# Feed-forward products in full float32 on unsplit activations, in place of two fp32r products on high and low parts

## What is computed

```python
def _L0_ffn_ref(x, W1, b1, W2, b2):
    def _ternary(w):
        scale = jnp.maximum(jnp.mean(jnp.abs(w)), 1e-08)
        w_t = jnp.clip(jnp.round(w / scale), -1.0, 1.0)
        return w + jax.lax.stop_gradient(w_t - w)
    h = jnp.einsum('bsd,fd->bsf', x, _ternary(W1)) + b1      # 256 -> 1024
    h = jax.nn.gelu(h, approximate=False)
    out = jnp.einsum('bsf,df->bsd', h, _ternary(W2)) + b2    # 1024 -> 256
    return out
...
x = x + _layernorm(_L0_ffn_ref(_layernorm(x, axis=-1), L0_ffn_W1, L0_ffn_b1, L0_ffn_W2, L0_ffn_b2), axis=-1)
```

## Time and profile before

| | us |
|---|---|
| median of 3 runs | 2201.29 (2200.94 to 2201.91) |
| the profiled execution | 2210.3 |
| its span, first to last instruction | 2208.5 |
| PE busy in the span | 1818.8 (82%) |
| DVE busy | 1532.1 (69%) |
| ACT busy | 863.3 (39%) |
| POOL (GpSimd) busy | 709.7 (32%) |

### The profile page before, as it was taken

How to read it: one execution, slowest core, us unless ns; L and a number is a source line. 1 busy time by engine, 2 the same in 40 slices (tenths; PEclk the granted TensorE clock), 3 DMA queues, 4 the chain that set the end, 5 groups by cost and what they waited for, 6 DMA issues and landing times. The chain is left out here.

```text
span 2208.5 us, 32795 instructions
## 1 busy us (share of the span) xinstructions
PE 1818.8 (82%) x10766; PEld 1165.7 (53%) x10766; DVE 1532.1 (69%) x3312; ACT 863.3 (39%) x1846; POOL 709.7 (32%) x643
## 2 busy tenths in 40 slices
PE   4878998898899889889988988998675654499977
PEld 2544555454555545545554555554444433489953
DVE  2346696598669668866965896697589845577736
ACT  1343353343335334433533343343422213366733
POOL 0000241043014104411420340143048863467641
PEclk9589999999999999999999999999876666699989
DMA  4000000000000000000000000000113234676667
GB/s 142 1 1 10 1 2 10 11 1 1 21 1 1 11 11 1 1 20 1 1 10 11 1 1 20 1 1 1 39 50 113 83 117 159 215 231 196 191 208 267
DMA packets 83443, 119.49 MB, mean 54 GB/s; under 512 B 12665, under 2 KB 70077, under 8 KB 83136
## 3 DMA queue, kind: packets, MB, share of 16 engines
q1 hardware_dynamic: 67088, 79.43, 11.4%
q0 software_dynamic: 13056, 35.68, 4.3%
q10 hardware_dynamic: 3120, 2.06, 0.3%
HBM read 67.43 MB, written 51.79 MB: 54 GB/s over the span
## 5 line engine op out<-in xcount | busy, mean ns | idle before, releaser
L681 DVE TENSOR_TENSOR_SCAN s_buf<-r_work,kvb 128x512 f32<-128x512 f32 x256 | 361.8, 1416 | 0.0
L866 POOL TENSOR_TENSOR p_buf<-s_buf,r_work 128x512 f32<-128x512 f32 x128 | 152.3, 1190 | 457.2 <-DVE s_buf L681 447.9
L956 ACT ACTIVATE probs<-bank_s,nmx 128x256 f32<-128x256 f32 (+1 forms) x512 | 186.9, 452 | 92.1 <-DVE nmx L541 90.5
L866 POOL TENSOR_TENSOR r_work<-s_buf,r_work 128x512 f32<-128x512 f32 x128 | 158.2, 1238 | 172.3 <-DVE s_buf L681 172.0
L821 POOL TENSOR_TENSOR rstd<-vare,mhalf 128x4 f32<-128x4 f32 x48 | 48.4, 1008 | 496.5 <-DVE vare L475 496.5
L974 ACT ACTIVATE pt<-bank_s 128x1024 f32<-128x1024 f32 (+1 forms) x128 | 117.6, 918 | 230.1 <-PE bank_s L1260 230.1
L670 DVE TENSOR_TENSOR kvb<-r_work,bank 128x512 f32<-128x512 f32 x256 | 174.2, 681 | 15.7 <-PE bank L1383 6.9
L1958 POOL DMA_INDIRECT y_rows<-w_in_ys,m_y_idx x144 | 141.9, 985 | 89.0 <-ACT w_in_ys L2046 52.2
L541 DVE TENSOR_REDUCE nmx<-bank_s 128x4 f32<-128x1024 f32 (+1 forms) x128 | 137.6, 1075 | 40.1 <-PE bank_s L1210 39.3
L1382 PE MATMUL bank<-v_hi,sel_v 128*128 128x512 f32 x256 | 130.2, 508 | 21.8 <-DVE kvb L670 15.4
L1210 PE MATMUL bank_s<-kT,qT 32*128 32x256 f32 (+1 forms) x1024 | 139.1, 391 | 0.0
(11 more groups left out here) (405 smaller groups left out, 4189.5 us busy)
## 6 DMA issues: line engine op xcount, KB each, us to landing
m_xs<-x_rows SPq DMA_DIRECT2D x144, 144.0 KB
w_lo<-y_rows SPq DMA_DIRECT2D x4, 2048.0 KB, 22.6
w_hi<-y_rows SPq DMA_DIRECT2D x4, 2048.0 KB, 24.9
w_in_ys<-in_w SPq DMA_DIRECT2D x17, 256.0 KB, 3.9
x_new<-in_x SPq DMA_DIRECT2D x8, 512.0 KB, 3.8
x_after_rwkv<-x_b SPq DMA_DIRECT2D x8, 512.0 KB, 3.7
m_x_all<-x_after_rwkv SPq DMA_DIRECT2D x8, 512.0 KB, 4.5
out<-m_x_all SPq DMA_DIRECT2D x8, 512.0 KB, 3.5
```

The lines of the kernel that those rows point to most:

```text
L681: V.tensor_tensor_scan(s_buf[:, n % 2, 1:S + 1], dec[:, n // HD, :], kvb[:, n % 2, :], 0.0, ALU.mult, ALU.add).then_inc(sem["state"], 1)
L866: G.tensor_tensor(p_slot(n), s_buf[:, n % 2, 0:S], rf[:, n // HD, :], ALU.mult).then_inc(sem["rs"], 1)
L956: ins = A(probs[:, n % 2, x, h * w:h * w + w], score_banks[n % 2][:, x, h * w:h * w + w], ACT.Exp, bias=nmx[:, n, 2 * x + h:2 * x + h + 1])
```

## The change

The weights stay in their tiles and are read as float32 (`bitcast(F32)`); the moving operand is unsplit float32. `up(f)` is now 2 products from `xT` (a float32 tile that attention uses earlier in the batch), `down(f)` 2 products. ACT writes `xT` in place of `hiT`, and its gelu goes straight to one of four slots in `work`, from which PE reads. DVE's `loT` and `g_lo`, ACT's `g_hi` and the semaphores `f_lo` and `g_lo` fall away: PE's first `up` waits for `evened`, and `down(f)` for `g_hi` of f, which the gelu now signals. A slot is written again when `down(f-4)` is done.

```diff
@@ vector
-                ve.wait_ge(sem["evened"], at(b, "evened", 4))
-                for k, src in enumerate((A0, A1)):
-                    ins = V.tensor_tensor(loT[:, k, :], src[:], hiT[:, k, :].bitcast(F32), ALU.subtract)
-                ins.then_inc(sem["f_lo"], 1)
                 yield "turn2"
                 for f in range(NF + 2):
-                    if f < NF:
-                        ve.wait_ge(sem["g_hi"], at(b, "g_hi", f + 1))
-                        V.tensor_tensor(g_lo[:, f % 2, :], work[:, f % 2, :], g_hi[:, f % 2, :].bitcast(F32), ALU.subtract
-                                        ).then_inc(sem["g_lo"], 1)
                     yield f"ffn{f}"
@@ scalar
-                    A(hiT[:, k, :], src[:], ACT.Copy).then_inc(sem["evened"], 1)
+                    A(xT[:, k, :], src[:], ACT.Copy).then_inc(sem["evened"], 1)
...
-                        if f >= 2:
-                            sc.wait_ge(sem["g_lo"], at(b, "g_lo", f - 1))
-                        g_ins = A(work[:, f % 2, :], bank[f % 3][:], ACT.Gelu, bias=b1[:, f:f + 1])
-                        g_ins.then_inc(act_own, 1)
-                        if f >= 2:
-                            sc.wait_ge(sem["f_y"], at(b, "f_y", f - 1))
-                        sc.wait_ge(act_own, b * NF + f + 1)
-                        A(g_hi[:, f % 2, :], work[:, f % 2, :], ACT.Copy).then_inc(sem["g_hi"], 1)
+                        if f >= 4:
+                            sc.wait_ge(sem["f_y"], at(b, "f_y", f - 3))
+                        A(g_slot(f), bank[f % 3][:], ACT.Gelu, bias=b1[:, f:f + 1]).then_inc(sem["g_hi"], 1)
@@ tensor, up
                     for k in range(NK):
-                        for c, part in enumerate((hiT, loT)):
-                            ins = T.matmul(bank[f % 3][:], w1t[:, k, f * P:(f + 1) * P], part[:, k, :],
-                                           start=k == 0 and c == 0, stop=k == NK - 1 and c == 1)
+                        ins = T.matmul(bank[f % 3][:], w1t[:, k, f * P:(f + 1) * P].bitcast(F32), xT[:, k, :], start=k == 0, stop=k == NK - 1)
@@ tensor, down
-                    pe.wait_ge(sem["g_lo"], at(b, "g_lo", f + 1))
+                    pe.wait_ge(sem["g_hi"], at(b, "g_hi", f + 1))
                     for k, dst in enumerate((A3, A4)):
-                        for c, part in enumerate((g_hi[:, f % 2, :], g_lo[:, f % 2, :])):
-                            ins = T.matmul(dst[:], w2t[:, f, k * P:(k + 1) * P], part, start=f == 0 and c == 0,
-                                           stop=f == NF - 1 and c == 1)
+                        ins = T.matmul(dst[:], w2t[:, f, k * P:(k + 1) * P].bitcast(F32), g_slot(f), start=f == 0, stop=f == NF - 1)
@@ tensor, before the first up
                 repeat(A4, 5)
-                pe.wait_ge(sem["f_lo"], at(b, "f_lo", 1))
+                pe.wait_ge(sem["evened"], at(b, "evened", 4))
```

More of the change, by code:

```diff
@@ L59 @@
     loc=QUADS, diff=QUADS, gate_z=1, gate_e=1, mixed=1, mixed_t=2, mixed_sb=2, out_ps=1,
-    f_lo=1, h_ps=NF, g_hi=NF, g_lo=NF, f_y=NF, fy_sb=2, fy_tok=1,
+    f_lo=0, h_ps=NF, g_hi=NF, g_lo=0, f_y=NF, fy_sb=2, fy_tok=1,
     r_var=2, r_rstd=2, r_normed=NT, r_turned=NK, r_xt=NK, mix=8, proj=8, v_f=2, v_lo=1, k_f=2, dec=2, decay=1, r_f=2,
@@ L172, in mid_token_layers @@
         s_zero = ctx.enter_context(nc.semaphore("s_zero"))
-        act_own = ctx.enter_context(nc.semaphore("act_own"))
         e_const = ctx.enter_context(nc.semaphore("e_const"))
@@ L307, in p_slot, with g_slot @@
             return p_buf[:, i, :] if i < 4 else r_work[:, (0, 1, 4, 5)[i - 4], :]
+        def g_slot(f):
+            return work[:, (0, 1, 4, 5)[f % 4], :]
         def at(b, name, k):
```

## The result

The changed kernel takes 2284.39 us (median of 4 runs, 2282.57 to 2287.42) against 2201.6 us for the kernel before; the ratio is 1.0365, with a 95% interval from 1.0345 to 1.0385, that is +82.8 us between the medians. Measured once more beside the experiments it took 2288.65 us (median of 6) against 2201.69, ratio 1.0387 (1.0347 to 1.0427), +87.0 us. The forecast was 2290.6 us, +89.3. Its sign, its mechanism and its range held. What remains to be explained are a few microseconds, and whether they lie in the terms of the sum or outside them.

What follows compares the result with a forecast made beforehand. PE was taken to bound the feed-forward stage: +103.7 us for products, -9.0 for the start and -5.4 for inner waits gave +89.3, a median of 2290.6 us. The range was 2277 to 2306 us.

Steps and rivals of the forecast that it cites:

- What bounds the stage: Feed-forward stage: PE's own time bounds it, busy 21.48 of 21.90 us in batch 2 at clock 1.00.
- The unit prices: Up and down products: 0.860 us per float32 product against 0.455 per fp32r pair, 256 times, 103.7 us more.
- Rival D: Up and down products: float32 with ternary weights needs no second record, deciding at 0.51 us a product; 2129 us, chance 0.03.
- The start: Start of the stage: without loT PE starts 1.1 us earlier each batch, 9 us back in all.
- Rival B: Stage start and g_lo waits: no wait comes back, PE stays held; +103.7, 2305 us, chance 0.06.
- The waits inside: PE's waits for g_lo before down vanish: 1.2 us back in batch 0, some 0.6 in each other, 5.4 together.
- ACT, DVE, slots, the end: Work freed on ACT and DVE, slot and bank waits, and the stage's last record: each worth nothing beyond the waits.
- The RWKV chain's cover: RWKV steps behind the fourth gelu, up to L1122: PE has 8.6 us of products meanwhile, so they cost nothing.
- The estimate by the pages: Products priced by the Trainium skill's pages: 110 us more for the products, 2297 us in all.
- The clock: Iterations outside the sum: losses of 12.3 us, placed at batch borders after PE idles, drawn anew; give or take 12 us.
- Rival A: Batch borders: the clock falls badly in every iteration, 28 us more, 2319 us; chance 0.06.

Runs made afterwards that it cites:

- after_act_dve_load: Changed kernel with ACT's rounding copy and DVE's subtraction of every gelu put back as work nobody reads or waits for: 2291.1 us, ratio 1.0388.
- up_f32: Kernel before with only the up products in float32 on xT, down and the gelu's parts as before: 2244.47 us, ratio 1.0173.
- down_f32: Kernel before with only the down products in float32 from the four slots, up and loT as before: 2244.35 us, ratio 1.019.
- high_only: Changed kernel with single fp32r products on the rounded activations, low parts left out of up and down: 2152.02 us, ratio 0.9746.
- after_start_wait: Changed kernel with DVE's unread loT subtraction put back and PE waiting for it before the first up: 2293.86 us, ratio 1.0427.
- before_filled: Kernel before with unread filler products in PE's two idle stretches at each batch's borders: 2205.08 us, ratio 1.0015.
- high_first: Kernel before with PE's terms reordered, high parts running before the waits for loT and g_lo: 2188.72 us, ratio 0.9933.

## Why the prediction was right, point by point

*What bounds the stage.* Right. PE is busy in 33.69 of 33.70 us, the clock is 1.00, and work put back on the other engines does nothing (after_act_dve_load), while passes of PE added or taken away come out in the stage (up_f32, down_f32, high_only).

*The unit prices.* Right: two records for each float32 product, 0.43 us apart, with weights of -1, 0 and 1 too. Rival D is out: its point of decision was 0.51 us a product, and the product takes 0.86.

*The start.* Forecast 1.1 us a batch, measured 1.14 after the change, 1.25 with the wait put back alone. PE starts where its fillers end, as predicted. Rival B would have left 1.38 and falls.

*The waits inside.* The one term that was mis-sized: I had 5.4 us in all; the stage grew by 94.65 and not by 103.7, so 9.0 came back. Most of the missing piece is visible in the trace of before. After each wait the next record starts 0.34 us behind the first and not 0.23:

```profile
581.56 0.50 PE L1313 MATMUL bank_s<-g_hi,w2t 128*128 128x512 f32 x1 [0.37 <-DVE g_lo L617]
...
581.90 0.39 PE L1313 MATMUL bank_s<-g_lo,w2t 128*128 128x512 f32 x1
...
582.13 0.39 PE L1313 MATMUL bank<-g_hi,w2t 128*128 128x512 f32 x1
```

A restart thus costs 0.11 us beyond the idle time. Each batch has three of them, the start and two waits, 0.33 us; I was off by 0.41 in batch 0 and by 0.46 in each other. (The second wait in the loop is short, 0.05 us.) The changed kernel has no restart because it has no wait: where one was put back, in after_start_wait, its float32 product lost 0.1 us in the same way. Of the 3.6 us in all, 2.6 are restarts and 0.4 is the pace, 0.429 us a record in the changed kernel and not 0.430; 0.6 is not accounted for.

*ACT, DVE, slots, the end.* All costed at nothing, and nothing is what they cost, as far as the stages tell: PE has no idle time in them. The RWKV chain's cover of 8.6 us was real: when high_only took it away, the wait appeared.

*The estimate by the pages.* An fp32r product in a row took 0.2275 us in the trace, where the Trainium skill ("TensorE: Matmul & The Clock Gate", section "Back-to-back issue gap") has 0.216. By that figure the estimate of the products' term was 110 us. The paces in the traces, 2 x 0.429 after and 2 x 0.2275 before, give 256 x 0.403 = 103 us, and the runs side with them.

*The clock.* I kept it out of the sum as something drawn anew and gave it 12 us in either direction; that was right in kind. Two things were not. I put the loss at the borders of batches, and before_filled shows that a clock held up there saves no time. Even in the longest iteration, the one of the earlier trace rows, the records at the border lost 5.79 - 3.70 = 2.1 us of the 5.75; the rest goes with a stretch further on, where the clock was low for 10 us:

```profile
1236.00:1246.20 10.20, 10.20 (x36) 5.33 (x35) 7.35 (x9) 1.50 (x5) 3.97 (x4) 0.51 0.00 0
```

And I called 0.2% what a measurement of this kernel can tell. The three runs that I had seen lay within 1 us; in later sessions executions of the same kernel before ranged from 2183 to 2216 us, and the intervals of the ratios are +-0.2 to 0.5%. Rival A (+28 us) did not come: the iterations of the changed kernel took 204.7 to 209.8 in its two traces, where I had named 205 to 211.

*Two slips.* The chances that I gave add up to 1.01. And three more iterations like the longest are 17 us, which ends at 2308 and so beyond the high end of 2306. Neither changes the forecast.

## What to carry to other kernels

A float32 product costs four passes of its moving columns where two fp32r products on a high and a low part cost two; the split is worth its extra work on the other engines as long as TensorE is the bound and they are not. Before removing a wait by changing the arithmetic, look at whether the order of the terms can hide it: starting with the high parts gave most of what the float32 version saved at the start of the stage (1.05 of 1.25 us a batch) and none of its passes. Price a stage by two cuts in the trace; they repeat to 0.05 us where the whole program moves by 1.5%. Set the cuts where PE does the same thing in both kernels: a record's start right behind another kind of work can be off by 0.2 us.

## What the runs showed of the hardware that I had not expected

- The same work in an iteration takes anything between 194 and 200 us, and some variants settle: up_f32's last six iterations all took 201.3 to 201.5 us, after_start_wait's 208.1 to 208.4, while the changed kernel, with 1.25 us less in each, wandered between 204.7 and 209.8. Work taken off an iteration does not come out one for one; a variant can look better or worse by several microseconds for this alone, in both directions (the iterations of high_only came out 12 to 18 us longer than its stages' 130 us would have it).
- The clock falls behind a stretch (L1193, products of 16 moving columns) in which TensorE's records touch and it counts as wholly busy, and six fillers of 512 columns spread through that stretch didn't prevent it: the program took 29 us more, of which 15 are the fillers' own time.
- Fillers in the idle stretches at the borders held the clock at 1.00 there (0.80 before) and left the median as it was, but the executions spread less: over 13 us and not 28 in the kernel before, over 17 and not 41 with the high parts first.
- After a wait, the second record starts 0.11 us later than in a row, with fp32r products (0.34 against 0.23 us, before) and with float32 ones (0.53 against 0.43, after_start_wait).
- The start of a record is not always the start of its work. An fp32r product behind a filler opens 0.04 us behind the filler's own start, and its successor follows 0.41 us later (high_first); a float32 product behind a filler opens 0.22 us behind it, and its successor follows 0.43 us later (after). Only the sum of the two distances can be compared.
